# Splitting the row maxima into three bf16 parts before they are turned, in a macaron block on one Trainium2 core

## The reference, cut to what matters

```
latent_kv = (k + v) @ W_down_kv
k_rec, v_rec = latent_kv @ W_up_k, latent_kv @ W_up_v      # per head
scores = einsum('bhqd,bhkd->bhqk', qh, k_rec) / sqrt(d)
scores = scores * exp(-0.01 * |t_q - t_k|)
attn = softmax(scores, axis=-1)
out = einsum('bhqk,bhkd->bhqd', attn, v_rec) @ W_o
```

## Time and profile before

| | |
|---|---|
| median of 3 runs | 6739.2 us (6736.05 to 6740.18) |
| the profiled execution: its time, its span | 6737.1 us, 6735.3 us |
| TensorE, VectorE busy | 83%, 71% of the span |
| ScalarE, GpSimd busy | 52%, 43% of the span |
| attention | about 1240 to 5490 us of the span |
| period of one pair | 26.5 us in the last batch, 26.5 to 41.6 us where the next batch is prepared |

### The profile page before, as it was taken

The page is one execution under the profiler, slowest core; times in us unless marked ns, Lnnn a source line. Parts: engine busy times, 40 slices in busy tenths (PEclk is TensorE's granted clock), DMA queues, the critical chain, the costliest instruction groups (busy, mean ns, idle before and its releaser), DMA issues.

```text
span 6735.3 us, 109029 instructions
## 1 busy us (share of the span) xinstructions
PE 5578.3 (83%) x35596; PEld 3237.8 (48%) x35596; DVE 4789.2 (71%) x10653; ACT 3487.3 (52%) x5077; POOL 2918.9 (43%) x2244
## 2 busy tenths in 40 slices
PE   5489993688888889889888898898889975499992
PEld 5478882233433344334333443343434445388872
DVE  7655552677877878778778788787787867555674
ACT  1134442366666666666666666666666651144431
POOL 6700004455445454554555555545545117600166
PEclk9999996799999999999999999999999985599996
DMA  5433332333333333333333333333333225333486
GB/s 175 160 99 105 105 104 84 89 96 94 101 96 95 96 99 94 94 97 99 94 96 92 102 96 89 103 93 94 99 91 94 71 68 184 143 101 104 134 262 217
DMA packets 573334, 741.96 MB, mean 110 GB/s; under 512 B 104434, under 2 KB 490612, under 8 KB 572788
## 3 DMA queue, kind: packets, MB, share of 16 engines
q1 hardware_dynamic: 523636, 600.70, 30.4%
q0 software_dynamic: 49152, 134.28, 6.1%
HBM read 441.30 MB, written 293.34 MB: 109 GB/s over the span
## 4 chain that ended last, share of the span: by engine, by line
PE 57%; DVE 16%; POOL 15%; issue 7%; ACT 4%; DMA 1%; SPq 0%; POOLq 0%; DVEq 0%; ACTq 0%
PE psum L1059 11%; PE psum L346 10%; PE psum L948 9%; PE psum L958 7%; POOL xs L617 7%; PE psum L363 5%; DVE at_mx L1187 4%; DVE at_Sd L1183 2%; POOL at_qs L1267 2%; DVE at_mp L1208 2%; PE psum L961 2%; DVE at_mp L1210 2%; PE psum L1037 2%; DVE at_mab L1191 2%; PE psum L335 2%
## 5 line engine op out<-in xcount | busy, mean ns | idle before, releaser
L1187 DVE TENSOR_REDUCE at_mx<-psum 128x4 f32<-128x512 f32 x3584 | 2224.1, 681 | 704.3 <-PE psum L948 704.2
L1131 ACT ACTIVATE at_P<-psum 128x1024 f32<-128x1024 f32 x2048 | 2036.1, 1021 | 867.6 <-PE psum L961 865.7
L948 PE MATMUL psum<-at_kst,at_qst 96*128 96x128 bf16 (+3 forms) x7168 | 1350.7, 298 | 402.7 <-DVE at_mx L1187 384.5
L948 PEld LDWEIGHTS psum<-at_kst,at_qst 96*128 96x128 bf16 x7168 | 557.2, 99 | 1344.2 <-DVE at_mx L1187 844.8
L958 PE MATMUL psum<-at_qst,at_kst 99*128 99x512 bf16 (+3 forms) x5120 | 1153.3, 324 | 29.7 <-ACT at_P L1131 27.7
L1059 PE MATMUL psum<-at_P,at_V 128*17 128x512 f32 x8192 | 1125.1, 622 | 0.0
L1279 POOL TENSOR_TENSOR at_Sd<-at_Sd,at_m 128x1024 f32<-128x1024 f32 x256 | 484.7, 1906 | 527.3 <-DVE at_m L1201 524.0
L958 PEld LDWEIGHTS psum<-at_qst,at_kst 99*128 99x128 bf16 x5120 | 478.5, 100 | 311.9 <-ACT at_P L1131 49.0
L1230 POOL DMA_INDIRECT at_xT<-ys,at_yib x256 | 245.7, 960 | 790.8 <-DMA at_gab<-table 709.4
L961 PE MATMUL psum<-at_ident,at_Sd 128*128 128x128 f32 x2048 | 572.9, 280 | 0.0
L1258 POOL TENSOR_TENSOR at_OT<-at_On,at_rc 128x128 f32<-128x128 f32 x256 | 98.3, 405 | 1004.2 <-DVE at_rc L1215 1004.2
(11 more groups left out here) (248 smaller groups left out, 8214.2 us busy)
## 6 DMA issues: line engine op xcount, KB each, us to landing
parts<-at_pt SPq DMA_DIRECT2D x768, 128.0 KB
at_qst<-parts SPq DMA_DIRECT2D x1536, 64.0 KB, 2.3
at_kst<-parts SPq DMA_DIRECT2D x256, 192.0 KB, 3.0
m2X<-xs SPq DMA_DIRECT2D x272, 128.0 KB, 2.0
ys<-m2X SPq DMA_DIRECT2D x272, 128.0 KB
m1X<-xs SPq DMA_DIRECT2D x264, 128.0 KB, 2.0
ys<-m1X SPq DMA_DIRECT2D x264, 128.0 KB
at_kst<-parts SPq DMA_DIRECT2D x256, 128.0 KB, 2.9
```

The lines of the kernel that those rows point to most:

```text
L948: ins = e.matmul(bank[(z + u) % 3][:, col - 512 * u:col - 512 * u + ln], self.qst[0:96, s, side, 128 * t:128 * t + 128], self.kst[0:96, s, ...
L1131: e.activation(self.P[:, i % NP, :], slot[a % 2], ACT.Exp).then_inc(self.taken.sem, 1)
L1187: e.tensor_reduce(self.mx[:, p % 2, hh, 8 * o + 4 * u:8 * o + 4 * u + 4], of, op=ALU.max, axis=AX.X).then_inc(self.s_read.sem, 1)
```

## The change

The three parts are made from at_m itself, on VectorE, right behind the instruction that joins it (item "max"): a cast to bf16, a subtraction, a cast, a subtraction, each on 128 partitions x 16 numbers, into at_mb (128 x 3 x 16). TensorE then turns all 48 columns in one bf16 matmul against a bf16 identity, ScalarE copies the 48x128 result once, with the sign changed, and SP sends 48 rows of 256 bytes out and brings them back as rows of 2 KB. Item "mlo" is gone from the list. The diff, without two unchanged lines that declare other tiles:

```diff
@@ -675,7 +675,8 @@
         self.mx, self.mab = sb("mx", [128, 2, 2, 56]), sb("mab", [128, 2, 16])
         self.m = sb("m", [128, 2, 16])
-        self.mT, self.mp = sb("mT", [16, 2, 128]), sb("mp", [16, 2, 3, 128], BF16)
+        self.mb, self.mr = sb("mb", [128, 2, 3, 16], BF16), sb("mr", [128, 16])
+        self.mp, self.identb = sb("mp", [48, 2, 128], BF16), sb("identb", [128, 128], BF16)
         self.rows = self.xT[:].rearrange("p k (t d) -> p (k t) d", d=D)
         ctx.close()
@@ -698,6 +699,7 @@
         self.s_filled, self.s_read = sig.new("a_s_filled", 32 * NPAIR), sig.new("a_s_read", 32 * NPAIR)
         self.shifted = sig.new("a_shifted", 2 * NPAIR)
         self.m_max, self.m_parts = sig.new("a_m_max", NPAIR), sig.new("a_m_parts", NPAIR)
+        self.ident_cut = sig.new("a_ident_cut", 1)
         self.weighed, self.ou_copied, self.shared = sig.new("a_weighed", 8 * NPAIR), sig.new("a_ou_copied", NPAIR), sig.new("a_shared", NPAIR)
         self.spread, self.inverse = sig.new("a_spread", B), sig.new("a_inverse", NPAIR)
         self.summed = sig.new("a_summed", 4 * B)
@@ -728,7 +730,7 @@
             score = (z // 8, self.ORDER[z % 8]) if z < 8 * NPAIR else None
             turn = (p, kb) if 0 <= s < 8 * NPAIR else None
             if split is not None:
-                yield from (("mlo", split), ("msend", split))
+                yield ("msend", split)
                 split = None
             if score or turn:
                 yield ("step", score, turn)
@@ -911,13 +913,12 @@
             if kind == "msend":
                 p = at[0]
                 s, z = p % NS, p % 2
-                w.wait_ge(*self.m_parts.at(p + 1))
-                e.dma_start(self.mdram[z], self.mp[:, z]).then_inc(self.m_out.sem, 16)
+                w.wait_ge(*self.result("mturn", p))
+                e.dma_start(self.mdram[z].rearrange("c h t q -> (c h t) q"), self.mp[:, z]).then_inc(self.m_out.sem, 16)
                 w.wait_ge(*self.m_out.at(16 * (p + 1)))
                 for hh in (1, 0):
                     for v in range(2):
-                        e.dma_start(self.qst[96:99, 2 * s + hh, v, :].rearrange("c (t q) -> c t q", q=128),
-                                    self.mdram[z, 8 * hh:8 * hh + 8].rearrange("t c q -> c t q")).then_inc(self.m_rows[s].sem, 16)
+                        e.dma_start(self.qst[96:99, 2 * s + hh, v, :], self.mdram[z, :, hh].rearrange("c t q -> c (t q)")).then_inc(self.m_rows[s].sem, 16)
             if kind == "res":
                 b, t2 = at
                 w.wait_ge(*self.x1_out.at(16 * (b + 1)))
@@ -1013,8 +1014,9 @@
                 ins.then_inc(self.filled.sem, 1)
             if kind == "mturn":
                 p = at[0]
-                w.wait_ge(*self.m_max.at(p + 1))
-                e.transpose(to[0:16, 0:128], self.m[:, p % 2, :], self.ident[:]).then_inc(self.filled.sem, 1)
+                w.wait_ge(*self.m_parts.at(p + 1))
+                w.wait_ge(*self.ident_cut.at(1))
+                e.matmul(to[0:48, 0:128], self.mb[:, p % 2].rearrange("p c n -> p (c n)"), self.identb[:], start=True, stop=True).then_inc(self.filled.sem, 1)
             if kind == "norm":
                 p = at[0]
                 w.wait_ge(*self.ou_copied.at(p + 1))
@@ -1107,8 +1109,7 @@
             if kind == "mturn":
                 p = at[0]
                 w.wait_ge(*self.m_out.at(16 * (p - 1)))
-                e.activation(self.mp[:, p % 2, 0, :], of[0:16, 0:128], ACT.Copy, scale=-1.0)
-                e.activation(self.mT[:, p % 2, :], of[0:16, 0:128], ACT.Copy, scale=-1.0).then_inc(self.taken.sem, 1)
+                e.activation(self.mp[:, p % 2, :], of[0:48, 0:128], ACT.Copy, scale=-1.0).then_inc(self.taken.sem, 1)
             if kind == "norm":
                 p = at[0]
                 w.wait_ge(*self.shared.at(p - 1))
@@ -1145,6 +1146,7 @@
         w.wait_ge(*self.loaded.at(176))
         e.tensor_tensor(self.wk[:], self.wk[:], self.wv, ALU.add).then_inc(self.w_ready.sem, 1)
         e.tensor_scalar_mul(self.wq[:], self.wq[:], 1.0 / 16.0).then_inc(self.w_ready.sem, 1)
+        e.tensor_copy(self.identb[:], self.ident[:]).then_inc(self.ident_cut.sem, 1)
         last, z = None, 0
         for kind, *at in self.plan:
             if kind == "stats":
@@ -1199,15 +1201,15 @@
                 if p >= 2:
                     w.wait_ge(*self.full("mturn", p - 2))
                 e.tensor_tensor(self.m[:, p % 2, :], self.mab[:, 0, :], self.mab[:, 1, :], ALU.max).then_inc(self.m_max.sem, 1)
-            if kind == "mlo":
-                p = at[0]
-                mT, mp = self.mT[:, p % 2], self.mp[:, p % 2]
-                w.wait_ge(*self.result("mturn", p))
-                k = own.end(e.tensor_tensor(mT, mT, mp[:, 0], ALU.subtract))
-                w.wait_ge(*k)
-                k = own.end(e.tensor_copy(mp[:, 1], mT))
-                w.wait_ge(*k)
-                e.tensor_tensor(mp[:, 2], mT, mp[:, 1], ALU.subtract).then_inc(self.m_parts.sem, 1)
+                m, mb, mr = self.m[:, p % 2, :], self.mb[:, p % 2], self.mr[:]
+                w.wait_ge(*self.m_max.at(p + 1))
+                k = own.end(e.tensor_copy(mb[:, 0], m))
+                w.wait_ge(*k)
+                k = own.end(e.tensor_tensor(mr, m, mb[:, 0], ALU.subtract))
+                w.wait_ge(*k)
+                k = own.end(e.tensor_copy(mb[:, 1], mr))
+                w.wait_ge(*k)
+                e.tensor_tensor(mb[:, 2], mr, mb[:, 1], ALU.subtract).then_inc(self.m_parts.sem, 1)
             if kind == "share":
                 p = at[0]
                 w.wait_ge(*self.result("norm", p))
@@ -1314,7 +1316,7 @@
         xs = nc.dram_tensor("xs", [XROWS, D], F32).ap()
         ys = nc.dram_tensor("ys", [NBLK * 128, D], F32).ap()
         parts = nc.dram_tensor("parts", [2, 2, H, 3, HD, 2, S], BF16).ap()
-        mdram = nc.dram_tensor("mdram", [2, 16, 3, 128], BF16).ap()
+        mdram = nc.dram_tensor("mdram", [2, 3, 2, 8, 128], BF16).ap()
         tables = [nc.dram_tensor(f"table{i}", [128, NT, 2], dt).ap() for i, dt in enumerate((U32, F32))]
         we = {"rw": rw, "rb": rb, "g": eg, "u": eu, "d": ed}
         wa = {"q": wq, "k": wk, "v": wv, "o": wo, "down": wdn, "upk": wuk, "upv": wuv}
```

## The result

The changed kernel takes 7088.98 us (median of 4 runs, 7086.86 to 7089.34), against 6738.57 us for the kernel before (4 runs): 1.052 times as long, 95% interval 1.0501 to 1.0538. The prediction was 7090. The profiled execution has a span of 7085.1 us, 349.8 more than before.

What follows compares the result with a forecast made beforehand. TensorE, with stalls behind VectorE's mlo, was taken to bound the attention. Added idle time of 240 and 24 us, 95 for the clock, less 10, make 349 on 6737: 7086, so 7090 us; 8-in-10 range 6830 to 7180.

Steps and rivals of the forecast that it cites:

- Mechanism and place: Behind the joined maximum, the new VectorE instructions on SBUF wait for GpSimd's running instruction; the join also releases both subs.
- The first rival: In the four new instructions only subtractions are shut out, 16-column casts pass freely: 6838 us, chance 0.11.
- the chain at which the sign turns: Length of the four new VectorE instructions behind the join at which slower becomes faster: about 3.4 us.
- The faster rival: Behind the join GpSimd gets in at most once among the four new instructions: 6540 or 6380 us, chance 0.08.
- Chain lengths: When the four new VectorE instructions end after the joined maximum at T: T+4.25 to T+6.2, by pair of a batch.
- Stalls: TensorE idling behind the four new instructions: 36.8 us per batch against 20.8 before, 240 us over 15 batches.
- the sum: Idle time 240 and 24 us, plus 95 for the granted clock, less 10 for minor effects: 349 us more.
- Clock: TensorE runs at the lower level (1.2 GHz) behind more long gaps: 95 us lost, bounds 30 and 180.
- The clean pair: Last-batch pair where GpSimd runs only the subs beside the new instructions; period to grow from 26.5 to about 30 us.
- Small parts: The bf16 turn may be shorter and one ScalarE copy is gone: 10 us off, between nothing and 35.
- Catching up: ScalarE's and GpSimd's stalls may hide in TensorE's new ones: up to 80 us beyond what was taken.

Runs made afterwards that it cites:

- The subs' extra wait: Changed kernel, but GpSimd's two subs wait for the three parts, not for the joined maximum alone: 6799.63 us, ratio 0.9611 to the kernel before.
- The matmuls in the stall: Changed kernel plus 14 unread matmuls ahead of the fill that waits for the four new instructions: 6974.19 us, ratio 1.0319 to the kernel before.
- one cast: Changed kernel, but VectorE makes only the first part, the second and third stay zero: 6721.39 us, ratio 0.9497 to the kernel before.
- the subs out of the way in the list: Changed kernel, subs waiting for the parts and both moved in the list to the turn's place: 6674.75 us, ratio 0.9425 to the kernel before.
- the first and third series: Follow-up measurement series in which the layers around the attention took about 2790 us instead of 2515; the kernel before took 7076.9 and 7083.2 us.
- memsets: Changed kernel, but a GpSimd memset replaces each sub, leaving out the diagonal scores: 6813.36 us in one run.

## Why the prediction held, step by step

**Mechanism and place: right, shown.** All three slow instructions end with an instruction of GpSimd. The subs' extra wait took the durations from 1.76, 1.81 and 1.28 to 0.175 us and turned the ratio from 1.052 to 0.961. The first rival, casts passing freely, is out: L1210 has the highest mean of the four, and a cast waits even for a memset. (Its sum also has an error: 8 pairs by 4.0 less 1.25 are 22, not 19, which gives 6841 and not 6838, and the chain at which the sign turns is then nearer 3.5 us.) The faster rival is out as well: GpSimd got in between each time. The prediction said that the two subs follow one another without a gap in all but two pairs of a batch; it is all but three, the third, the fourth and the sixth, which the chain lengths had right. That an indirect DMA shuts nothing out was assumed; 13 pairs of before bear it out, as told above.

**Chain lengths: right.** Ends were predicted from rows of before at T+5.8, 5.1, 5.1, 4.55, 6.2, 6.1, 4.25 and 5.8; they are 5.72, 5.08, 5.08, 4.51, 6.15, 5.94, 4.07 and 5.72. The changed kernel still had the same instruction of GpSimd behind the subs in each pair.

**Stalls: a little too large.** Predicted 36.8 us for the batch; the idle times in front of the late fill are 5.51, 4.26, 3.01, 4.30, 5.71, 5.83, 3.86 and 5.51, together 38.0, and less the 3.7 that the turn no longer waits in the fourth pair 34.3. "TensorE stalls for the chain's length to within 0.1 us" was the step that is off: the stall is 0.2 us shorter than the chain in the undisturbed pairs. The span shows the sum. TensorE is busy 5710.6 us of 7085.1, before 5578.3 of 6735.3: its idle time grew by 217.5 us, where 264 stood in the sum.

**Clock: too small.** TensorE's busy time grew by 132.3 us with the same 35596 matmuls, where 95 less 10 stood in the sum. By the clock's mean, 0.901 against 0.919, and two levels, it spent about 1403 us at the lower one (1.2 GHz) instead of 1091. The clean pair bears out the price of one gap: its period grew by 4.23, the stall by 2.62, which leaves 1.6 (1.5 assumed). Taking 110 down to 95 for gaps shorter than 5 us was the wrong way; what the 22 above 110 are is open. The matmuls in the stall show by another road that this is clock and not something else: they take 137 us out of the busy time, and the clean pair's clock goes back to 1.00.

**So the sum is better than its parts.** 349 against 349.8 measured is luck in its last digits: idle time 46 us too high, busy time 47 too low.

**Small parts: nothing, not 10.** The turn takes 0.302 us at the median where the float32 one took 0.277; at its fastest it is shorter (0.216 against 0.276), but it stands soon behind the new stall, mostly, as I read it, at the lower clock. The ScalarE copy is gone without effect on the end, and so are SP's wait and the shorter rows.

**Catching up: not seen.** Stalls might have let ScalarE and GpSimd get ahead, up to 80 us. A batch with preparation lost 21 to 23 us; 16.0 and a clock of 6.5 are 22.5. ScalarE's wait for GpSimd's scaling did fall, from 194.8 to 156.0 us, but that is in the shadow of the stall.

**The price of the faster rival: too good.** 6380 for short chains is a ratio of 0.947 and, less the 2515 outside, a stretch of some 3865 us; the wait alone gave 0.961 and 4004, and no chain but one cast 0.950 and 3926. Where VectorE no longer stops TensorE, ScalarE does in part, and my steps counted only the wait that went away. With the subs out of the way in the list, too, 0.9425 and 3877 are reached. Where the kernel before spent its extra time in the first and third series stays open, since no profile of it was taken there.

## What to carry to other kernels

Before putting small VectorE work with operands in SBUF on a path, look at what GpSimd runs at that moment and what the same event releases there: here four instructions worth 0.8 us took until 4.1 to 6.2 us behind the join, since the join released both. Order the two engines by a wait rather than let them meet, and then move what is held to a place in its queue where nothing useful stands behind it; the two together turned 5.2% slower into 5.8% faster, the move with some gain that may not depend on the change. Price each new gap of TensorE with the clock it loses behind it, here about 1.5 us for a gap of 4 to 5 us, on top of its length.

## What was not expected of the hardware

- Unread matmuls made a kernel faster: 1764 of them, 401 us of work, took 114 us off.
- A cast of 16 columns can't run beside a GpSimd memset (1.01 us instead of 0.17), while a subtraction of two SBUF operands can.
- The two engines took turns in the changed kernel: in all 128 pairs the subtraction L1208 took at least 1.76 us, none got through, although VectorE had run the first cast just before. With memsets the turns are not strict: a cast was passed over once in 15 pairs.
- Between series the kernel before differed by 5% (6739 and 7077 us); with the 2790 us that the other kernels showed there outside the attention, all but some 65 us of it lies outside. The cause is open: the first series, with 7077, and the second, with 6756, are on record with the same chip number.
